# Idle products of TensorE in the last network's edge pass of a four-network graph kernel

## What is computed

```python
h = jnp.maximum(_layernorm(x, axis=-1), 0.0)
qkv = h @ qkv_w + qkv_b                     # 6250 x (32 | 32 | 64), four heads
qe = q[s] * scale + (edge_attr @ q_rpe_w + q_rpe_b)
ke = k[t] + (edge_attr @ k_rpe_w + k_rpe_b)
ve = v[t] + (edge_attr @ v_rpe_w + v_rpe_b)
compat = einsum('ehd,ehd->eh', qe, ke)
ex = exp(compat - segment_max(compat, s)[s])
out = segment_sum(ve * ex / segment_sum(ex, s)[s], s)
x = x + out
```

## Time and profile before

| | |
|---|---|
| median of three runs | 13227.41 us |
| the profiled execution | 13221.39 us, of it 13219.6 us from its first to its last instruction |
| mean granted TensorE clock | 0.686 of full speed |
| network 3's edge pass | from about 11985 us (first ET) to 13187 us, 52 steps |
| busy in the span | PE 58%, DVE 60%, ACT 48%, POOL 67% |

### The profile page before, as it was taken

The page is one execution under the profiler, slowest core; times in us unless marked ns, Lnnn a source line. Parts: engine busy times, 40 slices in busy tenths (PEclk is TensorE's granted clock), DMA queues, the critical chain, the costliest instruction groups (busy, mean ns, idle before and its releaser), DMA issues. The chain is left out here.

```text
span 13219.6 us, 186410 instructions
## 1 busy us (share of the span) xinstructions
PE 7614.5 (58%) x46443; PEld 5797.6 (44%) x46444; DVE 7877.0 (60%) x21494; ACT 6293.1 (48%) x14084; POOL 8871.1 (67%) x9142
## 2 busy tenths in 40 slices
PE   5666455555531122335566666667665766657887
PEld 4666222222220012333456446544565455635665
DVE  8888666556642234334577667775767577754555
ACT  8333333233333324664466456545564465615665
POOL 0777677677767764776777677766776677736664
PEclk9766677777755555556677777778777877765555
DMA  0000111211121122224444444444444344412222
GB/s 32 2 2 2 36 39 39 35 40 39 39 37 40 40 32 52 53 53 78 120 128 126 95 125 127 126 103 116 129 125 109 107 129 126 115 36 65 64 66 56
DMA packets 820205, 951.09 MB, mean 72 GB/s; under 512 B 481321, under 2 KB 556636, under 8 KB 819432
## 3 DMA queue, kind: packets, MB, share of 16 engines
q0 software_dynamic: 343040, 637.31, 21.1%
q1 hardware_dynamic: 474344, 299.57, 8.4%
q10 hardware_dynamic: 2304, 9.46, 0.2%
HBM read 859.26 MB, written 86.39 MB: 72 GB/s over the span
## 5 line engine op out<-in xcount | busy, mean ns | idle before, releaser
L1659 POOL DMA_INDIRECT work<-t,idx x3328 | 3174.5, 954 | 1268.6 <-issue 1014.7
L803 POOL DMA_INDIRECT work<-t,idx x3328 | 3174.1, 954 | 1157.8 <-issue 1012.4
L815 ACT ACTIVATE work<-iota,loc 128x128 f32<-128x128 f32 (+1 forms) x6672 | 2034.2, 387 | 3498.2 <-DVEq L1109 1918.3
L1112 DVE TENSOR_TENSOR work<-work,ps 128x192 f32 x2496 | 882.8, 354 | 1229.2 <-PE ps L1136 932.5
L1136 PE MATMUL ps<-work 128*128 128x192 bf16 x2496 | 418.3, 308 | 1738.7 <-SPq L810 1665.9
L1754 PE MATMUL ps<-work 128*128 x6784 | 1328.3, 378 | 151.7 <-ACT work L828 96.3
L1754 PEld LDWEIGHTS ps<-work 128*128 128x128 f32 x6784 | 1310.1, 296 | 181.0 <-issue 160.6
L1766 PE MATMUL ps<-work 128*128 128x136 f32 x6656 | 1276.2, 350 | 12.1 <-DVE work L1820 9.8
L597 POOL DMA_INDIRECT tab<-work x784 | 850.7, 1085 | 588.3 <-DVE work L450 341.3
L725 POOL DMA_INDIRECT tab<-work x784 | 831.5, 1061 | 593.3 <-POOLq L39 360.3
L2618 POOL DMA_INDIRECT work<-t,idx x832 | 791.2, 951 | 555.5 <-issue 240.7
(11 more groups left out here) (417 smaller groups left out, 17046.0 us busy)
## 6 DMA issues: line engine op xcount, KB each, us to landing
work<-t,idx POOLq DMA_INDIRECT x7488
node<-pl SPq DMA_DIRECT2D x424, 256.0 KB, 3.4
work<-pl SPq DMA_DIRECT2D x54, 512.0 KB
work<-pl SPq DMA_DIRECT2D x106, 256.0 KB, 3.3
tab<-work POOLq DMA_INDIRECT x1568, 2.1
t<-work SPq DMA_DIRECT2D x196, 128.0 KB, 1.7
x<-work SPq DMA_DIRECT2D x196, 64.0 KB, 1.9
h<-work SPq DMA_DIRECT2D x28, 448.0 KB, 2.6
```

The source lines that it names most:

```text
L803: pool.indirect_dma_start(X[:, j % 4, n, :], None, table, bass.IndirectOffsetOnAxis(ap=idx[k][:, 8 * j + n:8 * j + n + 1], axis=0)).then_i ...
L815: t = act.activation(P[:, b, n, :], iota[:, :], ACT.Square, scale=-1.0, bias=loc[k][:, bass.ds(a + n, 1)])
L1112: added.on(dve.tensor_tensor(av, av, part(z, n), ALU.add))
L1659: pool.indirect_dma_start(X[:, j % 4, n, M - KD:W], None, table, bass.IndirectOffsetOnAxis(ap=idx[k][:, NT * j + n:NT * j + n + 1], axis=0 ...
```

## The change

In `views`, two products follow every tile (32 in a step). In `weigh_`, one follows every tile, for the fourth tile of a group behind the signal to VectorE (16 in a step). Each multiplies the bf16 identity (128 by 128) with the same identity shown four times side by side, so it has 128 rows and 512 columns, and writes the whole of bank `PS[0]`. Nothing reads the bank, and the products wait for no semaphore and signal none. Everything else stays.

```diff
+                def idle(pe, n):
+
+                    for _ in range(n):
+                        pe.matmul(PS[0][:, :].rearrange("p (a e) -> p a e", a=4), identb[:, :],
+                                  bc(identb[:, None, :], [128, 4, 128]), start=True, stop=True)
+
                 def views(pe, a, u, z):
...
                         if n % 4 == 3:
                             t.then_inc(qd.sem, 1)
+                        idle(pe, 2)
...
                     for n in range(4 * i, 4 * i + 4):
                         t = pe.matmul(part(n), P[:, b, n, :], MS[:, u, n, :], start=True, stop=True)
+                        if n % 4 < 3:
+                            idle(pe, 1)
                     t.then_inc(parts.sem, 1)
+                    idle(pe, 1)
```

## The result

The changed kernel takes 13395.24 us (median; 13387.15 to 13412.17) beside 13228.22 us of the kernel before: a ratio of 1.0131, 95% interval 1.0116 to 1.0146. The forecast was 13381 us. The profiled execution's span grew by 177.7 us, from 13219.6 to 13397.3.

What follows compares the result with a forecast made beforehand. Bound: a loop of PE from `factor` (12.13 us), ACT (9.85) and DVE (0.50), 22.48 us a step. Four steps take 105.3 us against 93.5, 11.8 more, x 13 groups = +154 us: 13381 us, range 13270 to 13540.

Steps and rivals of the forecast that it cites:

- F to the end of `turned` half 1: PE's work from `factor` (F) to the end of `turned` half 1: 13.3 us in place of 12.13.
- rival 4: Weight loads hide under idle products (0.11 us a `weigh_` tile), row changes halve: 13210 or 13197 us; faster, chance 0.08.
- F to ET: PE from `factor` to ET, which waits for DVE's scores: 22.9 us in place of 19.9.
- The ordinary step: A step away from the loop's end, PE's path plus ACT's 10.35 us: 23.7 us in place of 22.48.
- an ordinary step still ends by ACT: ACT's part, not PE's way to ET, ends an ordinary step: 22.9 + 0.65 is under 23.7 us.
- The loop's end: Each fourth step, where the loop goes round: 22.9 + 6.2 = 29.1 us in place of 26.0.
- The fall at the loop's end: Clock at half from `factor` after the loop goes round: a loss of 4.2 us once in four steps.
- the return at F + 9: After the loop goes round, the full clock returns 9 us behind `factor`, between 4 and 11.
- Falls at ordinary boundaries: Clock falls at boundaries between ordinary steps: 0.3 us added a step.
- rival 2: The clock never rises, so the products' 20.6 us a step come nearly in full: 14180 us; chance 0.04.
- rival 1: The clock falls at every step boundary, each step loses 4.2 us: +306 us, 13533 us; chance 0.18.
- rival 3: Row changes halve and the clock returns after 4 us: ordinary step 22.85 us, +60 us, 13285 us; chance 0.14.

Runs made afterwards that it cites:

- e4: The changed kernel with its idle products of one row in place of 128: 14607.68 us (one run).
- e5: e3 with 5 more idle products between `turned` half 0 and `factor`, 20 in the step after the loop's end: ratio 1.0008 to the kernel before.
- e3: The changed kernel with one idle product behind a tile of `views` in place of two: ratio 1.0169 to the kernel before.
- e8: e6 without its five idle products ahead of MX: ratio 1.0002; 1.0061 and 1.0057 on the chips where the kernel before was slow.
- e6: The changed kernel with most idle products moved into PE's waits, 29 a step: 13108.1 us, ratio 0.9911 to the kernel before.
- e7: The changed kernel with four more idle products behind `views` half 1, 52 a step: ratio 1.0127 to the kernel before.
- e9: e6 without the idle products inside `views`, 21 a step: ratios 1.0057 and 1.0032, both on chips where the kernel before was slow.

## Why the prediction was right

- **The mechanism:** as forecast, the clock rises and PE's path from F still gets longer, because what the products cost is a little more than what the full clock gives back. That the sum came out so near is in part luck, since its terms miss in both directions.
- **F to the end of `turned` half 1:** 13.3 us forecast, 13.38 measured. Errors cancel: `views` takes 6.73 us and not 6.50, the row transposes 0.36 and not 0.20, the three groups of `weigh_` 5.04 and not 5.35. The two changes of the number of rows in a tile of `views` still take 0.20 us together at the full clock (0.15 and 0.16 us between starts, where 128 columns stream in 0.053), all of what the earlier trace rows show, as the forecast had it. A tile takes 0.83 us and not 0.80 because its three products of 32 columns don't get faster: 0.09 us at the full clock (12683.08 to 12683.17), 0.10 before. A tile of `weigh_` takes 0.387 us, not 0.436, because the first fp32 record behind an idle product takes 0.06 us and not 0.11: less than in rival 4, which took 0.11 us off each tile.
- **F to ET:** 22.9 us forecast, 23.2 measured. MX at F + 13.6 agrees with F + 13.45 by two errors: by the forecast's own terms the column products begin at F + 10.6, and 3.25 us behind them is F + 13.9; they begin at F + 10.79, and MX follows 2.82 us behind.
- **The ordinary step:** 23.7 us forecast, 24.25 to 24.36 measured. The term that failed is "an ordinary step still ends by ACT". ACT's exponentials end at 12697.79 and VectorE's first product of the step stands 0.55 us later:

```profile
12697.49 0.30 ACT L2710 ACTIVATE work<-work 128x64 f32<-128x64 f32 x1
```
```profile
12697.43 0.28 DVE L2917 TENSOR_REDUCE work<-work 128x16 f32<-128x128 f32 x1
12698.34 0.42 DVE L2875 TENSOR_TENSOR work<-work,ps 128x256 f32<-128x256 f32 x1 [0.63 <-ACT work L2710]
```

  VectorE ends its scores at 12697.71 and needs 0.63 us before it starts `weighed`, though ACT is done 0.08 us behind the scores; by the program a load of 16 registers lies between, which the profile doesn't count as busy. e4 shows that this piece isn't ACT's: there the exponentials end at 12523.00, the scores at 12531.20, and `weighed` starts 0.62 us behind the scores (0.61 to 0.75 in its other ordinary steps):

```profile
12530.92 0.28 DVE L2917 TENSOR_REDUCE work<-work 128x16 f32<-128x128 f32 x1
12531.82 0.42 DVE L2875 TENSOR_TENSOR work<-work,ps 128x256 f32<-128x256 f32 x1 [0.62 <-issue]
```

  Before, it hid in the 2.20 us that VectorE waited for ACT. So PE's own way round, F to ET 23.2 (22.9 forecast) and 1.05 on, sets the step, and the sum left out the register load.
- **The loop's end:** 29.1 us forecast for the fourth step; 29.0 to 29.1 where the clock was up. But PE now stands 4.96 us on issue of its own before ET, the branch back of its sequencer (last section). It costs nothing: VectorE's scores end at 12618.30, its own pause on issue before `weighed` is 5.47 us, and F follows at 12624.24, 0.05 us behind `weighed`.
- **The fall at the loop's end:** 4.2 us forecast, 3.1 measured (16.43 - 13.38; single rounds 1.7 to 4.5). The term that was too large is the return at F + 9: the clock comes back 4.1 to 10.4 us behind F, at 7.1 on the mean. In the round that begins at F = 12730.62, one of the costliest, the stretch at half clock is (columns as in the earlier trace rows)

```profile
12730.62:12741.04 10.42, 10.42 (x44) 6.76 (x44) 4.46 (x19) 4.20 (x12) 3.73 (x4) 0.50 0.21 44
```

  and in one of the cheapest, from F = 12624.24, the tiles of `weigh_` 1 already follow each other in 0.39 us. Its rows at half clock and at full:

```profile
12627.17 0.53 PE L2801 MATMUL ps<-work 128*128 128x68 f32 x2
12627.50 0.64 PE L2770 MATMUL ps<-identb 128*128 128x512 bf16 x1
...
12628.85 0.34 PE L2801 MATMUL ps<-work 128*128 128x68 f32 x2
12629.02 0.38 PE L2770 MATMUL ps<-identb 128*128 128x512 bf16 x1
```

- **Falls at ordinary boundaries:** forecast 0.3 us a step. In seven of eleven rounds the clock fell behind F of the third or fourth step and cost 1.4 to 2.9 us: some 0.4 us a step. The stretch behind the fourth step's F at 12698.81 (columns as above):

```profile
12700.20:12710.30 10.10, 10.10 (x61) 5.66 (x61) 4.25 (x20) 3.51 (x11) 6.35 (x7) 0.67 0.25 56
```

- **The sum:** a round of four steps takes 106.6 us, where 105.3 was forecast; before it was 93.4. The ordinary step's error makes 1.8 us of the difference, the falls at ordinary boundaries 0.4 and the 0.3 that I took off 0.3 more; the cheaper fall at the loop's end takes 1.15 (4.2 - 3.05) back.
- **The rivals:** the clock did rise (against rival 2; e4 without its row changes is near the 40.9 us a step that I gave it), and fell at some ordinary boundaries, not at each (rival 1). The cheap ends (rival 3) and the gain (rival 4) fell with the row changes, which don't shrink. In e4 PE is 96% busy at 0.50. That contradicts again the Trainium skill's rule ("TensorE: Matmul & The Clock Gate", section "Why this matters for your kernels") that a continuously busy TensorE has the full clock. In e5, products in PE's waits keep the clock at 0.99 where e3 has 0.79. The Trainium skill says on the same page (section "HAM oscillation — how this bites in real kernels") that waits between bursts of matmuls take the clock away, and e5 agrees. The waits in its example are 3 to 5 us long, as PE's is at the loop's end; that one of 1.16 us decides is shown by the kernel of e8 alone.

## What to carry to other kernels

Before work is added to hold TensorE's clock, add up what the older work takes at the full clock, with pieces that don't scale (changes of the number of rows, other engines' parts of the loop) at their old price: here 12.1 us of PE's path became 13.4 us although the clock nearly doubled. Put such products first where the engine waits anyway: ten before one wait, five before another and a few in the thin parts gave a clock of 0.99 and a step of 19.9 us, where 48 inside the dense parts gave 0.93 and 24.3 us. The waits are also where the clock is lost, so one unfilled wait of 1.2 us can take back the gain. And a filled wait is free only while the clock stays up: ten products took 2.2 us of it in e6 and up to 4.1 us at half clock in e8, where they then held up the work behind them.

## What was not expected of the hardware

- TensorE's sequencer has 982 instructions in a round of the loop (weight loads and its own among them; 790 before) and takes 4.3 to 5.2 us from its branch back to the next instruction, against 0.27 us with 790, 854, 898, 918 and 953 in other kernels here. With 998 in e7 it takes 3.6 to 4.5 us. In e4, also with 982, it takes 3.4 to 4.1 us in ten of eleven rounds and 7.2 in one, but PE still has products queued meanwhile, so ET comes only 0.7 to 1.4 us later in the ten. Where between 953 and 982 it begins, and why, was not tried.
- An fp32 record of 68 columns takes 0.06 us of the full clock behind a 512-column product and 0.11 us behind its like. The weight load of the first starts together with the wide product (12686.73) and is over when the record starts (12686.94); that the load is what makes the difference was not tried.
- A change of the number of rows between bf16 products (119 to 55, 55 to 128) adds 0.10 us each at either clock (0.20 and 0.22 us from start to start at half, 0.15 and 0.16 at full).
- On two chips the kernel before takes 19200 and 18658 us where it takes 13215 to 13228 on the others. VectorE's scores start there only behind the gathers' last packets, 14 us and more behind TensorE's products, and the steps of 39 us hid what e8 and e9 were to tell.
